# A graph network kernel: product and row sum of edge features, as two large VectorE instructions or as eight fused ones

## What is computed

```python
h = x @ Wn.T + bn
e = edge_attr @ We.T + be                       # edge_attr: 100000 x 128
a = leaky_relu(sum((h[src] + e) * attn, axis=-1))
a = exp(a - segment_max(a, dst)[dst])
out = relu(segment_sum(h[src] * a / segment_sum(a, dst)[dst], dst))
```

## Time and profile before

| what | value |
|---|---|
| median of 3 runs | 4699.41 us |
| their spread | 4694.25 to 4701.1 us |
| the profiled execution's own time | 4693.42 us |
| its span in the profile | 4691.6 us |
| VectorE busy, share of the span | 58% |
| TensorE busy, share of the span | 76% |
| first loop, by the trace | 97 to 705 us |
| second loop, by the trace | 733 to 1765 us |

### The profile page before, as it was taken

One profiled execution on the slowest core, in us unless ns is written; L12 is line 12 of the kernel. 1 busy time (PEld: TensorE's weight loads), 2 busy tenths in 40 slices (PEclk: granted clock), 3 DMA queues, 4 the chain that ended last, 5 costly groups with the idle time before them and its releaser, 6 DMA issues. The chain is left out here.

```text
span 4691.6 us, 87142 instructions
## 1 busy us (share of the span) xinstructions
PE 3560.4 (76%) x19416; PEld 2666.4 (57%) x19417; DVE 2729.4 (58%) x7745; ACT 1686.2 (36%) x5377; POOL 1202.6 (26%) x828
## 2 busy tenths in 40 slices
PE   5555557888887767999983333589999699998978
PEld 4333335777776666888862222577888444444444
DVE  7999999999987771112237777677766300000523
ACT  1444442234444440000017776577776100000110
POOL 1888888888888100000000000000000000000000
PEclk9999999999998888999985555899999899999989
DMA  2333333567767664444445544343332153442064
GB/s 102 102 102 102 101 97 86 149 177 209 218 204 241 243 237 120 134 120 144 134 112 173 162 157 151 121 140 123 117 97 76 36 208 129 160 153 79 1 249 137
DMA packets 435571, 656.93 MB, mean 140 GB/s; under 512 B 97532, under 2 KB 291767, under 8 KB 435362
## 3 DMA queue, kind: packets, MB, share of 16 engines
q1 hardware_dynamic: 354306, 526.63, 36.2%
q10 hardware_dynamic: 53040, 121.95, 7.2%
q0 software_dynamic: 28144, 7.36, 2.5%
HBM read 438.84 MB, written 216.02 MB: 140 GB/s over the span
## 5 line engine op out<-in xcount | busy, mean ns | idle before, releaser
L989 POOL DMA_INDIRECT slots<-all_B,put_index x800 | 1179.2, 1474 | 345.7 <-issue 240.8
L1725 POOL DMA_DIRECT2D out_dram<-all_B x7 | 8.5, 1221 | 2242.2 <-DVE all_B L1709 2242.2
L965 PE MATMUL put_ps<-put_right_in,put_left_in 128*128 128x125 f32 x2380 | 351.6, 298 | 138.6 <-ACT put_left_in L835 138.2
L765 DVE TENSOR_SCALAR put_hot<-all_iota_bf,put_words_in 128x125 bf16<-128x125 bf16 x2400 | 445.3, 315 | 3.3 <-DMA put_words_in<-slots 3.3
L1220 PE MATMUL lm_ps<-lm_v,lm_node 125*128 x1220 | 170.0, 184 | 328.4 <-DVEq L1087 127.3
L1185 ACT ACTIVATE lm_raised<-lm_hot,srt_words 128x125 f32<-128x125 bf16 x1200 | 360.3, 385 | 140.2 <-DVE lm_top L1100 64.6
L965 PEld LDWEIGHTS put_ps<-put_right_in,put_left_in 128*128 128x128 f32 x2380 | 307.1, 204 | 167.8 <-ACT put_left_in L835 157.4
L835 ACT CAST put_left_in<-put_hot 128x640 f32 (+1 forms) x238 | 172.5, 725 | 629.6 <-issue 321.8
L2262 DVE TENSOR_TENSOR upd_pre<-upd_po,upd_bias 125x512 f32<-125x512 f32 x25 | 17.3, 692 | 630.5 <-PE upd_po L2193 630.5
L1835 PE MATMUL att_ps<-att_right,att_left 128*125 128x125 f32 x2380 | 318.7, 286 | 68.4 <-ACT att_right L1856 64.6
L969 PE MATMUL put_ps<-put_right_out,put_left_out 128*128 128x125 f32 x2380 | 342.7, 297 | 0.0
(11 more groups left out here) (346 smaller groups left out, 5955.9 us busy)
## 6 DMA issues: line engine op xcount, KB each, us to landing
c_T<-counts SPq DMA_DIRECT2D x255, 312.5 KB, 2.9
pair<-put_T ACTq DMA_DIRECT2D x125, 625.0 KB
hot<-put_hot SPq DMA_DIRECT2D x480, 160.0 KB
att_ring<-hot SPq DMA_DIRECT2D x240, 320.0 KB, 3.2
all_A<-in_edge_attr_dram SPq DMA_DIRECT2D x100, 448.0 KB
lm_planes<-src_rows SPq DMA_DIRECT2D x123, 320.0 KB, 3.7
counts<-put_T ACTq DMA_DIRECT2D x125, 312.5 KB
lm_hot<-hot SPq DMA_DIRECT2D x120, 320.0 KB, 3.0
```

The source lines that it names most:

```text
L765: ins = v.tensor_scalar(hot[:, h, t, c * S:c * S + P], k["iota_bf"][:, :], words_in[:, j, c, t:t + 1], None, ALU.is_equal)
L965: ins = t_.matmul(tile(1, c), left_in[:, c, :], right_in[:, c, :], start=False, stop=False, skip_group_check=True)
L989: nc.gpsimd.indirect_dma_start(slots, bass.IndirectOffsetOnAxis(index[:, C * g + j:C * g + j + 1], 0), stage[:, C * g + j, :], None).then_ ...
```

## The change

The two instructions of `edge_dot` become eight. Each takes one edge of the eight in every partition, 128 columns: it multiplies them with `vrow`, writes the product to `prod`, and sums it; the sum goes to one column of `dot`. The wait for `staged`, which stood between product and sum, now stands ahead of all eight. The semaphore `multiplied` is gone: SP's load of the features, two groups on, waits for `dotted`, which the last of the eight raises, where it waited for the product alone. The shapes, the buffers, the loops and everything else are as before.

```diff
                         sp.dma_start(planes[NB * t:NB * t + NB, h, :], plane[ds(g, 1), :].to_broadcast([NB, CP])
                                      ).then_inc(blocks_in[h], 16)
-                        sp.wait_ge(multiplied, g - 1 + HEAD)
+                        sp.wait_ge(dotted, g - 1 + HEAD)
                         for rows_of in EVEN:
...
                 def edge_dot(i, u):
                     g, h = 4 * i + u, u % 2
                     dve.wait_ge(loaded[h], 32 * (2 * i + u // 2) + 32)
-                    v.tensor_tensor(prod[:, h, :, :], ea[:, h, :, :], f["vrow"][:, :].unsqueeze(1).to_broadcast([P, C, DE]),
-                                    ALU.mult).then_inc(multiplied, 1)
-                    dve.wait_ge(multiplied, g + 1 + HEAD)
                     dve.wait_ge(staged, g - 3 + HEAD)
-                    v.tensor_reduce(dot[:, u, :], prod[:, h, :, :], AX.X, ALU.add).then_inc(dotted, 1)
+                    for c in range(C):
+                        ins = v.tensor_tensor_reduce(prod[:, h, c, :], ea[:, h, c, :], f["vrow"][:, :], 1.0, 0.0, ALU.mult, ALU.add,
+                                                     dot[:, u, c:c + 1])
+                    ins.then_inc(dotted, 1)
```

More of the change, by code:

```diff
@@ L528, in phase_front @@
         blocks_in, loaded = [b.sem(f"blocks_in{h}") for h in range(2)], [b.sem(f"loaded{h}") for h in range(2)]
-        based, cols_hot, rows_hot, multiplied, dotted, picked, placed = (
-            b.sem(n) for n in ("based", "cols_hot", "rows_hot", "multiplied", "dotted", "picked", "placed"))
+        based, cols_hot, rows_hot, dotted, picked, placed = (
+            b.sem(n) for n in ("based", "cols_hot", "rows_hot", "dotted", "picked", "placed"))
         counted, carried, negated, looked = (b.sem(n) for n in ("counted", "carried", "negated", "looked"))
@@ L677, in turn @@
                             place(chain, i, 0)
-                for sem in (rows_hot, cols_hot, multiplied, dotted, picked, placed):
+                for sem in (rows_hot, cols_hot, dotted, picked, placed):
                     dve.sem_inc(sem, HEAD)
```

## The result

| | before | after |
|---|---|---|
| median of 4 runs | 4696.83 us | 4636.31 us |
| their spread | 4693.02 to 4701.1 | 4633.92 to 4638.13 |
| profiled execution's span | 4691.6 us | 4635.9 us |
| first loop, first `row_hots` to first table | 96.4 to 708.7 us | 96.3 to 658.1 us |

The ratio is 0.9871 with a 95% interval from 0.9853 to 0.9888: 60 us or 1.3% faster. The forecast was 13.5 us faster, with a range from 4668 to 4746; the measured time lies 32 us under its lower end.

The account below looks back on a forecast made before the run. VectorE's queue was taken to pace the first loop. Eight pairs at -0.165 us plus a 0.03 us charge gave -0.135 us a group, -13.5 us in 100 groups: 4699.4 to 4686 us, range 4668 to 4746.

Parts of the forecast that it names:

- The bound: First loop: VectorE's queue sets the pace, and a shift there moves everything behind it one to one.
- The slack of 1.26 us: TensorE's look-up ends before `pick` starts, so up to 1.26 us of gain could be used in the tight groups.
- The product's price: Dot product: a fused 128-column product takes 0.215 us from its start to the accumulator read's start.
- The read's price: Dot product: each accumulator read costs VectorE's queue 67 ns before the next product, at most 0.142 us.
- the lower bound, 2.09 us: Eight pairs in a group at the cheapest: 8 x (0.194 + 0.067) us for product and read.
- The charge for the issue of the next wait: Ahead of `pick`: register steps no longer hidden behind the long sum, 0.03 us a group, ends 0 and 0.06.
- the second failed step: GpSimd's scatters beside the new pairs: no charge, since two-source instructions are not held; scatter's end has 226 us of cover.
- what would make it wrong: First loop: VectorE's gaps in other places of the turn growing by what the dot product gives back.
- The load: SP's features load is issued up to 1.1 us later, within some 8 us of cover, so at no cost.
- hold the queue: Rival, dot product: next product starts only after the read, pair 0.357 us, +46 us; chance 0.17 for +20 to +46.
- the 0.26 of slower issue: Rival, dot product: fused instructions start 0.26 us apart before the read, +22 us, 4721 us; chance 0.12.
- the 0.35 of half the rate: Rival, dot product: fused instruction takes two cycles a column, 0.35 us, +94 us, 4793 us; chance 0.05.

Follow-up runs that it names:

- e2_twice: Changed kernel with every fused instruction run twice, the first time into spare tiles that nobody reads: 4881.52 us, ratio 1.0198, first loop 743.8 us.
- e1_builtin: Changed kernel with its eight fused instructions written as the older product with accumulator (scalar_tensor_tensor): ratio 0.9857, first loop 569.3 us.
- e5_pick: Changed kernel with `pick`'s two products and its sum also written as eight fused instructions of 50 columns: 4637.64 us, ratio 0.9855, first loop 554.9 us.
- e11_apart: Kernel before, with the sum over 1024 columns moved behind `pick`, apart from its product: 4688.04 us in one run, first loop 601.5 us.
- e7_before_late: Kernel before, with GpSimd's scatters held back until the first loop is over: 4980.37 us in one run, first loop 605.3 us.
- e8_after_late: Changed kernel, with GpSimd's scatters held back until the first loop is over: 4903.06 us in one run, first loop 532.8 us.
- e4_wait_only: Kernel before, with only SP's load of the features waiting for the sum instead of the product: ratio 1.0000, first loop 612.2 us.
- e10_both_again: Changed kernel with `pick` as eight fused instructions and `place`'s three one-source steps given a second source: 4624.25 us, ratio 0.9849, first loop 542.1 us.
- e3_place: Changed kernel with the three one-source instructions of `place` (lines 658 to 660) given a second source: ratio 0.9833, first loop 554.6 us.

## Why the prediction was wrong

**The bound** was read right. VectorE's queue sets the first loop's pace: with every pair twice the loop became longer by all of it (e2_twice). The slack of 1.26 us that `pick` had was enough.

**The product's price** was right: 0.215 us from product to read, 0.2125 measured. It came from line 2366 and the step per column.

**The read's price failed**, and with it the sum. The prediction took 67 ns, "of a short instruction in a full queue only a part counts", from the spacing of line 2281's small instructions. Measured, it is nothing: the next product starts with the read (after, and e1_builtin). 8 x 0.067 = 0.54 us a group, 54 us in the whole, four times the forecast gain. The same row 2366 was read for what it showed, product to read, and a stand-in was taken for what it did not show, read to follower. The honest lower end of that price was zero, and it was not in the range: the lower bound, 2.09 us, was made with 67 ns for the read as well. With zero, the lower end would have been 8 x 0.194 = 1.55 us, -0.87 us a group, and the range would have held the result.

**The charge for the issue of the next wait**, 0.03 us, was not needed: `pick` starts with the last read. Nor did it show behind the fused pick, where the gap is the 0.14 us that stood behind the sum as well (e5_pick).

**GpSimd** was the second failed step. It was taken to cost nothing, because the two-source instructions of the new row would not be held. They are not: line 637 took 273 to 353 ns, with a median of 277. But what stood elsewhere in the turn was. The prediction saw that something in the old pair kept GpSimd out (it named the product and the sum; e11_apart shows the product alone to be at work) and that line 621 could be stretched; it did not ask where the scatters would fall once they were no longer kept in step with the pair. 22 us of 72 were given back in lines 658, 659, 619 and 621 (e7_before_late, e8_after_late). It had named such a growth of other places as what would make it wrong.

**The sum again.** The first loop was forecast 13.5 us shorter. The read and the charge that were not there, and the product's few ns, made it 59 us more, 72.5; GpSimd's holds took 22 back, which leaves 50.5. The two errors have opposite signs: had GpSimd's holds not grown, the forecast would have been further off. Nor is the sign to the forecast's credit by much: it gave 0.40 to faster and 0.38 to slower.

**The load** that is issued later costs nothing (e4_wait_only), as said.

**The rivals** on the slower side did not come. The reads do not hold the queue. At 0.2125 us from product to product there is no room for the 0.26 of slower issue or the 0.35 of half the rate. The Trainium skill's sentence on two fp32 sources (Vector Engine (DVE) Microarchitecture Reference, Points that are easy to get wrong) does not hold here, neither for the older form (e1_builtin, 0.21 us for 128 columns) nor for the new one.

**What is left over.** The first loop explains 50.5 us. The profiled spans differ by 55.7 and the medians by 60.5. Behind the first loop the program is the same one: the second loop took 6 us more (1032.7 against 1026.7) and all behind it 11 us less (2919.9 against 2931.2). The second loop's length goes with the mean clock granted in it, whichever dot product ran before: 1026.7 us at 0.925, 1032.7 at 0.920, 1041 at 0.907 (e10_both_again), 1100 at 0.884 (e3_place), 1154 at 0.863 (e4_wait_only). What sets that clock is not shown. Behind the second loop the clock is the same in all, 0.88, and the length still varies from 2920 to 2932 us, for a reason that I did not find. The 10 us are not shown to belong to the change.

## What to carry to other kernels

Where an engine's queue sets the pace, price an instruction by the distance to the next start, and where no row shows what follows it, let the range run from zero to its whole length. Here a fused product with sum and a read of the accumulator cost the queue 0.21 us at 128 columns, and eight of them (1.70 us) beat one large product and one large sum (2.425 us). When an instruction that kept another engine out is replaced, look for the next one that the other engine can now catch: here a TENSOR_SCALAR step of 16 columns went from 0.2 to 0.6 us. And when one instruction ends just as another does, check which of them the held one always ran beside: the end pointed at the sum, the cause was the product.

## What the runs showed of the hardware

- The read of VectorE's accumulator adds no time from start to start. It starts with the next product behind it, in the older form and in the newer one. Product to product is 0.2125 us for 128 columns from SBUF (after, e1_builtin) and 0.13 us for 50 columns from PSUM (e5_pick): by these two, an estimate, about 0.08 us for each instruction and 1.06 ns for each column.
- While GpSimd issues its scatters, TENSOR_SCALAR steps of VectorE, with one source, are held for up to 0.4 us. Steps with two sources are stretched by 0.08 us at most (line 637 in the changed kernel), and a sum with one source not at all (line 651: 569 to 572 ns in 100 cases). The same step took 570 ns with one source and 175 with two (e3_place); with no scatters beside it, it took 174 with one (e8_after_late).
- A scatter instruction is 1.19 us long by itself. Beside a product of two fp32 sources over 1024 columns it was stretched to up to 3.4 us, until the end of the next sum; beside the sum over 1024 columns alone it took 1.18 to 1.20 (e11_apart, 96 cases); beside rows of fused pairs it took 1.39 in the mean and 2.09 at most.
- The second loop took 1027 us at a mean granted clock of 0.925 and 1154 us at 0.863.
